# Selection matrices built three or four per instruction, and thinner waits around the gathers, in a one-core GNN kernel

## The reference

```python
# network 0: two relational layers
seg = dst * N_REL + rel
agg = segment_sum(h[src], seg).reshape(N_ENT, N_REL, -1)
out = relu(einsum('nri,rio->no', agg, W) + h @ loop_w + bias)   # W = einsum('rb,bio->rio', w_comp, basis)
# network 1: two attention layers, 4 heads of 32, self loops added
xw = (x @ W).reshape(n, H, FH)
e = leaky_relu(al_s[src] + al_d[dst], 0.2)
ee = exp(e - segment_max(e, dst)[dst])
out = segment_sum((ee / segment_sum(ee, dst)[dst]) * xw[src], dst) + b
h = elu(batch_norm(out))
```

## Time and profile before

| | |
|---|---|
| time, median of 3 runs | 4555.91 us (4553.63 to 4557.06) |
| the profiled execution, from first to last instruction (span) | 4547.9 us |
| time less span | 8.0 us |
| busy: GpSimd, TensorE, VectorE, ScalarE | 3132.4, 3121.2, 2544.8, 1107.5 us |
| indirect DMAs on GpSimd | 1564 at L2081, 1660 at L2098 |
| mean granted clock of TensorE | 0.649 |

### The profile page before, as it was taken

One profiled execution on the slowest core, in us unless ns is written; L12 is line 12 of the kernel. 1 busy time (PEld: TensorE's weight loads), 2 busy tenths in 40 slices (PEclk: granted clock), 3 DMA queues, 4 the chain that ended last, 5 costly groups with the idle time before them and its releaser, 6 DMA issues.

```text
span 4547.9 us, 63220 instructions
## 1 busy us (share of the span) xinstructions
PE 3121.2 (69%) x13439; PEld 2273.6 (50%) x13439; DVE 2544.8 (56%) x9924; ACT 1107.5 (24%) x2623; POOL 3132.4 (69%) x3271
## 2 busy tenths in 40 slices
PE   7976777777756666666646676767674666676766
PEld 3444444444434444444435555656563555565655
DVE  6534444444434455555556566767674667676776
ACT  3311222222200111111122233323332223332333
POOL 1057777777767777777677777777727777777772
PEclk9966889888855555555555566656665556665666
DMA  6633444444432222222222222222212222222222
GB/s 232 259 111 98 151 148 154 149 150 154 154 97 62 65 65 65 66 66 66 61 54 54 54 54 54 54 54 54 54 39 58 55 55 55 55 54 54 54 55 73
DMA packets 168049, 394.03 MB, mean 87 GB/s; under 512 B 57414, under 2 KB 92036, under 8 KB 150532
## 3 DMA queue, kind: packets, MB, share of 16 engines
q0 software_dynamic: 103616, 215.16, 17.9%
q10 hardware_dynamic: 37536, 102.42, 6.0%
q1 hardware_dynamic: 26532, 72.39, 4.3%
HBM read 229.57 MB, written 160.17 MB: 86 GB/s over the span
## 4 chain that ended last, share of the span: by engine, by line
PE 39%; DMA 15%; DVE 14%; issue 13%; POOL 11%; ACT 4%; DVEq 2%; SPq 1%; ACTq 0%; POOLq 0%
DMA Gr<-Ttab,GID 12%; PE B L1837 11%; PE B L1979 8%; POOL Gr L2098 8%; PE B L1737 6%; PE B L1799 3%; POOL Gr L2081 3%; DMA Gr<-Gtab,SRC 3%; DVE XA L1128 2%; DVE XA L935 2%; DVE Sr L1027 2%; PE B L1911 1%; PE B L1895 1%; ACT hold L1534 1%; DVE Gr L1103 1%
## 5 line engine op out<-in xcount | busy, mean ns | idle before, releaser
L2098 POOL DMA_INDIRECT Gr<-Gtab,SRC x1660 | 1603.1, 966 | 584.2 <-issue 448.5
L2081 POOL DMA_INDIRECT Gr<-Ttab,GID x1564 | 1497.3, 957 | 604.6 <-PE B L1837 272.8
L1837 PE MATMUL B<-Gr,Sr 128*128 x3328 | 999.0, 410 | 596.5 <-SPq L2114 328.6
L1837 PEld LDWEIGHTS B<-Gr,Sr 128*128 128x128 f32 x3328 | 731.3, 270 | 1051.9 <-issue 1036.4
L1979 PE MATMUL B<-Gr,Sr 128*128 128x136 f32 x3328 | 959.3, 432 | 132.9 <-DVE XA L1128 80.9
L1979 PEld LDWEIGHTS B<-Gr,Sr 128*128 128x128 f32 x3328 | 740.3, 295 | 203.7 <-DVE XA L1128 130.3
L935 DVE TENSOR_TENSOR XA<-XA,B 128x128 f32 x1664 | 471.6, 283 | 571.8 <-PE B L1837 521.3
L1128 DVE TENSOR_TENSOR XA<-XA,B 128x136 f32 x1664 | 480.8, 289 | 294.2 <-PE B L1979 237.9
L924 DVE TENSOR_SCALAR Sr<-iota,DL 128x128 f32<-128x128 f32 x1664 | 493.3, 300 | 20.6 <-issue 16.2
L1737 PE MATMUL B<-XA,H 128*128 128x512 f32 x664 | 412.5, 709 | 1.7 <-DVE H L602 0.4
L1027 DVE TENSOR_SCALAR Sr<-iota,DL 128x128 f32<-128x128 f32 x1664 | 370.2, 295 | 0.0
(11 more groups left out here) (287 smaller groups left out, 3001.2 us busy)
## 6 DMA issues: line engine op xcount, KB each, us to landing
Ttab<-Sr ACTq DMA_DIRECT2D x83, 1024.0 KB, 4.2
Ttab<-Sr SPq DMA_DIRECT2D x51, 1024.0 KB, 3.9
Gr<-Gtab,SRC POOLq DMA_INDIRECT x1660
Gr<-Ttab,GID POOLq DMA_INDIRECT x1564
Gtab<-Gr ACTq DMA_DIRECT2D x83, 66.0 KB
X1D<-Gr ACTq DMA_DIRECT2D x83, 64.0 KB
out<-Sr SPq DMA_DIRECT2D x12, 256.0 KB
Gtab<-XA SPq DMA_DIRECT2D x5, 528.0 KB, 3.8
```

Of the source, the lines that this page charges most:

```text
L1837: e.matmul(B[banks[s % len(banks)]][:, 0:P], selr(s), Gr[:, bass.ds(o, P)], start=True, stop=True).then_inc(slot_mm, 1)
L2081: e.indirect_dma_start(out=Gr[:, (sn + 1) % TG * P:((sn + 1) % TG + 1) * P], out_offset=None, in_=Tt[L][:, :], in_offset=bass.IndirectOffs ...
L2098: e.indirect_dma_start(out=Gr[:, (s % GR) * CW:(s % GR) * CW + 132], out_offset=None, in_=T2[L][0:NPAD][:, :], in_offset=bass.IndirectOffs ...
```

## The change

Five things are changed together.

1. Relational layers, VectorE: in place of one `tensor_scalar` of 128 columns per slot there is one `tensor_tensor` of 384 columns in every third step, over three neighbouring places of the ring, comparing `iota` (repeated three times by a stride of 0) with three columns of `DL` (each repeated 128 times by a stride of 0). `built_v` is counted for the first two sets of a layer only.
2. Attention layers, VectorE: in place of four `tensor_scalar` there is one `tensor_tensor` of 512 columns. `sel_made` counts sets of four.
3. TensorE, relational layers: the wait for `landed[L]` is carried by the matmul itself and no longer by an instruction of its own ahead of it.
4. GpSimd: the waits for `slot_mm` and `gat_mm` are made with every fourth gather only, for the slot that the last of the four needs.
5. SyncE: `landed[L]` is raised by two after each pair of tiles, once both have landed.

```diff
+BACK = 4
+SB3, FIRST_SETS = 3, 2
@@ build @@
+        def selections(e, s, n, ring):
+            o = s % ring * P
+            return e.tensor_tensor(Sr[:, o:o + n * P].rearrange("p (s d) -> p s d", d=P),
+                                   iota[:, :].unsqueeze(1).to_broadcast([P, n, P]),
+                                   DL[:, s:s + n].unsqueeze(2).to_broadcast([P, n, P]), ALU.is_equal)
@@ vector @@
-                    if sn < NS:
-
-                        e.tensor_scalar(out=selr(sn), in0=iota[:, :], scalar1=DL[:, sn:sn + 1], scalar2=None,
-                                        op0=ALU.is_equal).then_inc(built_v, 1)
+                    if sn < NS and sn % SB3 == 0:
+                        ins = selections(e, sn, min(SB3, NS - sn), SRR)
+                        if sn // SB3 < FIRST_SETS:
+                            ins.then_inc(built_v, 1)
@@ gat_vector, prep @@
-                        for s in range(c0 + 4 * k, c0 + 4 * k + 4):
-                            e.tensor_scalar(out=sel(s), in0=iota[:, :], scalar1=DL[:, s:s + 1], scalar2=None,
-                                            op0=ALU.is_equal).then_inc(sel_made, 1)
+                        selections(e, c0 + 4 * k, 4, SR).then_inc(sel_made, 1)
@@ gat_scalar, prep @@
-                        e.wait_ge(sel_made, L * NS + c0 + 4 * g + 4)
+                        e.wait_ge(sel_made, (L * NS + c0) // 4 + g + 1)
@@ tensor @@
-                            e.wait_ge(built_v, L * NS + s + 1)
-
-                        e.wait_ge(landed[L], kregs[s % 32 // 16][s % 16])
+                            e.wait_ge(built_v, L * FIRST_SETS + s // SB3 + 1)
+
                         o = off(e, pregs[s % 32 // 16][s % 16], (TG - 1) * P)
-                        e.matmul(B[banks[s % len(banks)]][:, 0:P], selr(s), Gr[:, bass.ds(o, P)], start=True, stop=True).then_inc(slot_mm, 1)
+                        ins = e.matmul(B[banks[s % len(banks)]][:, 0:P], selr(s), Gr[:, bass.ds(o, P)], start=True, stop=True)
+                        ins._wait_ge(landed[L], kregs[s % 32 // 16][s % 16])
+                        ins.then_inc(slot_mm, 1)
@@ gpsimd @@
-                    if back >= 0:
-                        e.wait_ge(slot_mm, L * NS + back + 1)
+                    last = min(back + BACK - 1, NG - 1 - TG + NS - NT)
+                    if back >= 0 and (back % BACK == 0 or sn == 0):
+                        e.wait_ge(slot_mm, L * NS + last + 1)
...
-                    if s >= GR:
-                        e.wait_ge(gat_mm, L * NS + s - GR + 1)
+                    if s >= GR and s % BACK == 0:
+                        e.wait_ge(gat_mm, L * NS + min(s + BACK, NGS) - GR)
@@ relay @@
-            for t in range(NG):
+            for t in range(0, NG, 2):
                 wait_gather(e, L * NG + t)
-                e.sem_inc(landed[L], 1)
-            for t in range(NG, NT):
-                e.sem_inc(landed[L], 1)
+                wait_gather(e, L * NG + t + 1)
+                e.sem_inc(landed[L], 2 if t + 2 < NG else 2 + NT - NG)
```

## The result

The changed kernel takes 4622.95 us (median of 4 runs, 4620.37 to 4626.25), the kernel before beside it on the same chip 4554.77 us (4551.56 to 4557.06): a ratio of 1.015, with a 95% interval from 1.0138 to 1.0162. It is slower. Forecast were 4614 us and a range from 4576 to 4647. The profiled execution has a span of 4621.6 us where the kernel before has 4547.9, a difference of 73.7; between the medians it is 68.2.

The account below looks back on a forecast made before the run. GpSimd issuing gathers was taken to bound the kernel; new stalls +74, old stalls -17 and pairs +1 gave +58, so a span of 4605.9 us, and with 8.0 us around it 4614 us; range 4576 to 4647 us.

Parts of the forecast that it names:

- What bounds the kernel: Four gather stages: GpSimd issuing gathers one after another, 0.955 us median plus a 0.30 us pause, sets the pace.
- GpSimd's fewer waits: GpSimd's product waits, made every fourth gather: 0 us, since the waits cost nothing and none for products appears.
- fourth rival: GpSimd's thinner waits shorten the 0.30 us pause by 0.03 us, 73 us less, about 4541 us; 3 in 100.
- Pairs: Relational layers, landed tiles counted by twos: two products are left at a layer's end instead of one, adding 1 us.
- The stall: kind and law: A gather starting under a VectorE tensor_scalar or two-SBUF-input instruction loses the rest of it less 0.12 us.
- first rival: A tensor_tensor doesn't stop a gather: 16.9 us of old stalls go, none come, 4539 us; 6 in 100.
- The stall: its size: Gathers under wide selections: new stalls of 43 us at 512 columns and 31 at 384, together 74 us.
- The formula: With random starts, a VectorE instruction of length d costs the gathers (d - 0.17)^2 / (2 x 1.26) on average.
- old stalls: Gathers held under the single-column selections of the kernel before: 17 us, which go with the change.
- replay of the old trace: Each selection group in the trace replaced by one long instruction at the first's place: 15, 8, 30, 36 us by stage.
- bound of +91: Upper end of the whole change's cost, with each chunk's stalls at their upper end: 107 - 17 + 1 us.
- second and third rivals: Gather-selection phases settle well or stalls balance, about 4556 us, 5 in 100; or settle badly, about 4660 us, 6 in 100.

Follow-up runs that it names:

- e1b: The changed kernel with selections made one per instruction again (tensor_scalar, 128 columns), fewer waits and pairs kept: 4553.03 us beside 4553.72 for the kernel before.
- e8: The kernel before, with the first scan of an attention stage reading its scores in PSUM, not the SBUF copy: 4550.86 us beside 4553.72 for the kernel before.
- e9: The changed kernel with attention selections made eight at a time (1024 columns) in place of four: 5561.01 us beside 5565.51 for the kernel before.

## Why the prediction was right

*What bounds the kernel.* Right. The stages are GpSimd's own time with 0.30 us between gathers, and each grew by what the gathers grew: 1005.4, 1004.6, 1074.8 and 1069.0 us where 1002, 1000, 1074 and 1064 were forecast. The mean of a gather is 987 ns in the attention layers and 981 in the relational ones, for 983 and 975.

*GpSimd's fewer waits, 0 us.* Right; e1b shows it on the clock. No wait for a product is over 0.3 us in the changed kernel either, and the smallest distance between a product and the gather that reuses its slots is 7 us there (6.5 before). The fourth rival falls.

*Pairs, 1 us.* The stretches between and behind the gathers are 26.2, 13.5, 85.3 and 83.9 us, 3.5 us more than the earlier trace rows. In the profile of e8, which keeps the old counting, the same stretches come to some 2 us more than in the earlier trace rows, so that a microsecond can't be told from the scatter between two executions. Not contradicted, not shown.

*The stall: kind and law.* Right. A gather that starts under an instruction with both operands in SBUF loses what is left of it less 0.12 us, at 256, 384, 512 and 1024 columns (for nine in ten of the held gathers of the changed kernel and of e9 it is the rest less 0.124 to 0.132 us). The exceptions, starts in the first hundredths and two instructions without a gap, are told of below. Here the first rival was decided, and it falls. The Trainium skill (page "SBUF — State Buffer", section "Who interferes with whom") lets a `tensor_tensor` with two SBUF inputs contend only with what GpSimd reads, and infers that the writing of a DMA's descriptors is left alone. That this frees a gather is what the runs speak against: 429 gathers began under such selections and lost 85.5 us. A gather of this kernel also reads its row numbers from SBUF (`GID`, `SRC`), so that the rule itself may stand and only the inference fail; no run here tells which of its accesses is the one that waits. The same section holds that with at most one SBUF input, outside the two-port modes, VectorE doesn't contend with GpSimd. Here the trace agrees for the selections: -0.7 and 0.0 us of excess in the stage with the indices in PSUM. It doesn't for the memsets told of below, which have no SBUF input and held gathers.

*The stall: its size.* This is the term that was mis-sized. New stalls were to be 43 us under 512 columns and 31 under 384, together 74; they are 46.2 and 39.3, together 85.5. The formula had been called sound since it gave 15 us for old stalls of 16.9. That was partly luck: it gives 7.5 us for either pair of layers, and the trace has 14.4 in the attention layers and 2.5 in the relational ones. Two parts:

- The lengths. The two shapes take 0.686 and 0.555 us on average, not 0.680 and 0.545. By the same formula that makes 44 and 33 us.
- The starts are not at random, and this is the rest of the 8 us for 384 columns. Of the 248 gathers that began under one, 119 had 0.40 us or more left; with starts spread evenly over 0.555 us it would be 28%, 69 of them. The forecast's replay of the old trace gave 15, 8, 30 and 36 us for the four stages; they had 19.2, 20.0, 22.6 and 23.6. Its sum of 89 is near only because its errors cancel. A likely reason is that a longer selection moves the landings that the next one follows, which the replay left out; no run was made for it.

The old stalls (17 us) went as said, the first scan's rose from 5.9 to 7.2, and those under L588 (now L596) fell from 3.8 to 1.0. The sum that was forecast as +58 is +73.7 on the spans, within the bound of +91. The median is 9 us over the forecast, 0.2%, and part of this nearness is luck. The span of 4605.9 us that was forecast is 15.7 too short; but 8.0 us were added for what lies around a span, and that is 1.8 us in the changed kernel's profiled execution (4623.42 beside 4621.6) and 1.9 in e1b's (4554.06 beside 4552.2). The other 6 us look like scatter: with 1.8 us around its span of 4547.9 the profiled execution of the kernel before would have taken 4549.7 us, less than each of the three times that the forecast started from. The second and third rivals (phases that settle well, or badly) both fall, the time being between them.

## What to carry to other kernels

Before making an instruction wider to save an engine's time, ask who else waits for its ports: where GpSimd's indirect DMAs set the pace, what VectorE does from two SBUF operands costs by the square of its length, (d - 0.17)^2 over twice the gather's period here, and a lighter VectorE can make a slower kernel. One operand in PSUM takes the cost away at the same width; where none can be, many short instructions with a gap between them hold the gathers for less than one long one (17.5 us beside 46.2; the gain in time was not seen). A releaser named in the profile for an idle time that is the same with and without the wait is only a name: compare the lengths of the pauses before thinning the waits.

## What the runs showed of the hardware that I had not expected

- *Two in a row can act as one.* Two wide selections that follow without a gap can hold a gather through both (0.32 us lost with 0.11 left; 51 gathers of 129), with a gap of 0.07 us they don't (none of 91): 36.2 against 17.5 us.
- *A memset holds a gather, too, and an instruction can do so that begins later.* The gather at 2331.13 took 2.31 us, 1.35 too many. A memset on 128 partitions began 0.14 us behind it, and a wide selection behind that one ended at 2332.62; the rest less 0.12 is again the loss (1.49 - 0.12 = 1.37). One more gather met such a memset 0.14 us behind its start and lost 1.34, and one that began 0.09 us behind a memset's start lost 1.11 (a rest of 1.25 to the end of the selection behind it); thirteen others had theirs 0.22 us or more behind the start and lost next to nothing. In the kernel before the nearest of this kind began 0.17 us behind a gather and cost nothing. In e1b a memset of 833 columns on one partition began 0.10 us behind a gather, which lost 1.60 us. Not every memset does it: short ones (132 columns on one partition, 0.17 us) that began 0.01 us behind a gather cost nothing in either kernel. So what a gather needs, it seems to ask for some 0.12 to 0.15 us after its start, which would also be the "less 0.12". This is a reading of few cases; no run was made for it.
- *The first hundredths of a microsecond can go either way.* The 30 gathers that began with 0.55 us or more left of a 384-wide selection lost nothing, and the selection took up to 0.07 us longer (0.62 in place of 0.55, at 321.38). Of the 16 with 0.64 us or more left of 512 columns 13 lost nothing and three 0.52 to 0.54 us. What decides it isn't known.
- *The same kernel can take a fifth longer in another session*, with the gathers and VectorE's and ScalarE's instructions as long as ever and pauses between them that no row explains, and two changes of a per cent change their sign. A verdict on waits or on widths holds for the bound under which it was measured.
